# First attention stage: the next head's transposes moved to mid-head and to other PSUM banks, weightings placed between root tiles, three root tiles ahead of the log tiles

## The reference

```python
q, k = _l2norm(to_heads(q)), _l2norm(to_heads(k))
cos = jnp.einsum('bhsd,bhtd->bhst', q, k)
g_dist = jnp.arccos(jnp.clip(cos, -1.0 + EPS, 1.0 - EPS))
attn_score = (1.0 + g_dist) ** (-3.2)
n_r, n_c = jnp.sum(attn_score, axis=-1), jnp.sum(attn_score, axis=-2)
k_tilde = (n_r ** -1.0)[..., :, None] * attn_score * (n_c ** -1.0)[..., None, :]
probs = k_tilde / jnp.maximum(jnp.sum(k_tilde, axis=-1, keepdims=True), 1e-12)
out = jnp.einsum('bhst,bhtd->bhsd', probs, v)
```

## Time and profile before

| | |
|---|---|
| runs, us | 3973.3, 3965.14, 3962.1 (median 3965.14) |
| profiled execution, us | 3964.4 |
| its span, us | 3962.6 |
| mean granted TensorE clock | 0.802 |
| busy over the span | PE 80%, DVE 75%, ACT 80%, POOL 30% |

### The profile page before, as it was taken

One profiled execution on the slowest core, in us unless ns is written; L12 is line 12 of the kernel. 1 busy time (PEld: TensorE's weight loads), 2 busy tenths in 40 slices (PEclk: granted clock), 3 DMA queues, 4 the chain that ended last, 5 costly groups with the idle time before them and its releaser, 6 DMA issues. The chain is left out here.

```text
span 3962.6 us, 59670 instructions
## 1 busy us (share of the span) xinstructions
PE 3159.4 (80%) x18880; PEld 1315.8 (33%) x18880; DVE 2984.2 (75%) x4684; ACT 3180.3 (80%) x2658; POOL 1175.7 (30%) x746
## 2 busy tenths in 40 slices
PE   4777787778777877787777575888888888888899
PEld 2221122112211221122111232355555555555547
DVE  6777977797779777977797798878787787788411
ACT  2699999999999999999998564488788787888822
POOL 2111011101110111011100043477677676777700
PEclk8776677667766776677667698799999999999999
DMA  1000000000000000000000135011001000110000
GB/s 38 32 7 7 0 6 6 6 0 6 6 6 2 5 6 6 4 3 6 6 5 5 35 124 154 22 39 28 23 23 44 23 23 23 39 28 23 18 19 11
DMA packets 59591, 86.13 MB, mean 22 GB/s; under 512 B 9808, under 2 KB 45904, under 8 KB 58960
## 3 DMA queue, kind: packets, MB, share of 16 engines
q1 hardware_dynamic: 59344, 83.06, 7.4%
HBM read 52.44 MB, written 30.54 MB: 21 GB/s over the span
## 5 line engine op out<-in xcount | busy, mean ns | idle before, releaser
L1089 POOL TENSOR_TENSOR lo<-pr,hi 128x1024 f16<-128x1024 f32 x384 | 916.7, 2412 | 396.9 <-ACT hi L1215 394.8
L1138 DVE TENSOR_REDUCE mx<-mx_ps 128x1 f32<-128x512 f32 x1024 | 660.1, 684 | 175.1 <-PE mx_ps L1253 171.8
L660 PE MATMUL r_ps<-qst,kst 72*128 72x512 bf16 x1024 | 575.6, 565 | 252.2 <-DVE wt L470 188.9
L1230 ACT ACTIVATE pr<-s_ps 128x1024 f32<-128x1024 f32 x512 | 531.6, 1038 | 275.4 <-PE s_ps L1274 243.8
L664 PE MATMUL r_ps<-mst 110*128 110x512 f16 (+1 forms) x1024 | 512.7, 507 | 81.5 <-DVE wt L451 35.4
L1215 ACT ACTIVATE hi<-pr 128x1024 f16<-128x1024 f32 x512 | 547.3, 1070 | 0.0
L287 POOL COPY mono_x<-two 128x256 f32 (+1 forms) x16 | 8.5, 530 | 1781.4 <-PE t_ps L633 1727.9
L1253 PE MATMUL mx_ps<-ka,qa 128*128 128x512 f16 x1024 | 385.3, 397 | 139.3 <-DVE mx L1138 116.4
L589 ACT ACTIVATE wt<-wt 128x2048 f32<-128x2048 f32 x256 | 484.6, 1895 | 0.0
L580 ACT ACTIVATE wt<-wt,theta_bias 128x8192 f32<-128x8192 f32 x64 | 453.6, 7111 | 0.2
L1293 PE MATMUL pv_ps<-vh,hi 128*128 128x129 f16 x4096 | 434.2, 223 | 11.3 <-ACT sums L1221 5.8
(11 more groups left out here) (179 smaller groups left out, 4302.6 us busy)
## 6 DMA issues: line engine op xcount, KB each, us to landing
qk<-stg SPq DMA_DIRECT2D x6, 2048.0 KB, 13.6
vh<-v SPq DMA_DIRECT2D x16, 520.0 KB, 3.6
qa<-qk SPq DMA_DIRECT2D x16, 512.0 KB, 3.7
ka<-qk SPq DMA_DIRECT2D x32, 256.0 KB, 4.8
v<-v_st SPq DMA_DIRECT2D x3, 2080.0 KB, 7.9
qst<-parts_dram SPq DMA_DIRECT2D x144, 32.0 KB
kst<-parts_dram SPq DMA_DIRECT2D x144, 32.0 KB
qk<-stg SPq DMA_DIRECT2D x4, 1024.0 KB, 8.3
```

Of the source, the lines that this page charges most:

```text
L660: mm = eng.matmul(r_ps[:, r % 2, :], kst[:, cols(k)], qst[:, cols(n_, BANK)], start=True, stop=True)
L1089: eng.tensor_tensor(lo[:, i % NHL, :, :], pr_slot(i), hi[:, i % NHL, :, :], ALU.subtract).then_inc(lo_done, 1)
L1138: eng.tensor_reduce(mx4[:, q // NCH, q % NCH:q % NCH + 1], mx_ps[:, q % 2, :], AX.X, ALU.max)\
L1230: eng.activation(pr_slot(i), s_ps[:, i % 2, :, :], ACT.Exp, scale=SM).then_inc(exp_done, 1)
```

## The change

It moves work between places of each engine's order, in the first attention stage alone; no instruction is taken out, and ScalarE gets two more `theta` calls a head (six groups where there were four, over the same tiles).
- **Order of tiles.** The ring and VectorE take three root tiles, then the eight log tiles, then five root tiles (before: four, eight, four).
- **Factors.** `turn_factors` writes into `m_ps`, whose two halves are free between a head's last square and the next head's first; so its 32 transposes no longer wait for VectorE's copies one by one. They stand behind the tenth ring chunk of the fourth root tile. `turn` stands behind the tenth chunk of the third root tile of the next head.
- **Weightings.** Places 0, 1 and 2 stand behind the tenth ring chunk of root tiles 5, 6 and 7 (the last three, counted from 0); places 3 to 8 between the ring's end and `start`; places 9 to 13 behind `start`; 14 and 15 open the next head, as before.
- **VectorE.** `values` of places 0 to 3 stands behind root tile 4, that of places 4 to 7 behind root tile 6. The four `stack` copies follow root tile 7. `finish` and `finish_rows` of the head before move to the third root tile.
- **Theta groups** are of 4, 4, 5, 1, 1 and 1 tiles.
- **`ring_to`** is worked out from other constants.

```diff
+    RA = 3
+    GROUPS = (0, 4, NL, NL + 5, NT - 2, NT - 1, NT)
+    PAIRS = tuple(range(0, NL, 2)) + (NL,)
...
-    ROOT_US, CHUNK_US, HALF_US = 1.035, 0.69, 1.24
+    ROOT_US, CHUNK_US, CUBE_US, LOAD_US, LAG_US = 0.954, 0.625, 2.35, 1.3, 1.2
...
-        st_ps = t_ps[:, :, :].rearrange("p a b -> p (a b)").bitcast(F16)
+        st_ps = m_ps[:, :, :].rearrange("p a b -> p (a b)").bitcast(F16)
...
                     if not first:
-                        values(h - 1, NT - 2, 2)
-                    for j in range(QH):
+                        values(h - 1, NT - 2, 1)
+                        values(h - 1, NT - 1, 1)
+                    for j in range(RA):
+                        if j == RA - 1 and not first:
+                            finish(h - 1)
                         root_tile(h, j)
+                    if not first:
+                        finish_rows(h - 1)
                     for j in range(NL):
                         log_tile(h, j)
-                    for j in range(QH, NQ):
+                    for j in range(RA, NQ):
                         root_tile(h, j)
-                    if not first:
-                        finish(h - 1)
-                    values(h, 0, GROUPS[1])
-                    values(h, GROUPS[1], NL - GROUPS[1])
-                    if not first:
-                        finish_rows(h - 1)
+                        if j == NQ - 4:
+                            values(h, 0, GROUPS[1])
+                        if j == NQ - 2:
+                            values(h, GROUPS[1], NL - GROUPS[1])
                     if not last:
                         for j in range(4):
                             stack(h + 1, j)
-                    values(h, NL, QH)
-                    values(h, NL + QH, QH - 2)
+                    values(h, NL, GROUPS[3] - NL)
+                    values(h, GROUPS[3], NT - 2 - GROUPS[3])
...
                     for r in range(done, NRING):
                         ring(h, r)
-                    if not first:
-                        turn(h - 1)
-                    for p in range(NL):
-                        weigh(h, p)
-                    if not last:
-                        for j in range(4):
-                            turn_factors(h + 1, j)
-                    for p in range(NL, NL + QH):
+                        if r == q_at(RA - 1) + 9 and not first:
+                            turn(h - 1)
+                        if r == q_at(RA) + 9 and not last:
+                            for j in range(4):
+                                turn_factors(h + 1, j)
+                        for p in range(3):
+                            if r == q_at(NQ - 3 + p) + 9:
+                                weigh(h, p)
+                    for p in range(3, NL + 1):
                         weigh(h, p)
                     if not last:
                         start(h + 1)
-                    for p in range(NL + QH, NT - 2):
+                    for p in range(NL + 1, NT - 2):
                         weigh(h, p)
```

More of the change, by code:

```diff
@@ L324, in stage_attention0 @@
     NCU = 2 * NQ
[L325 removed]
+    NSG = len(PAIRS) - 1
     def q_at(j):
[L328 removed]
+        return 12 * j if j < RA else 12 * j + 4 * NL
     def s_at(j):
[L331 removed]
+        return 12 * RA + 4 * j
     def place(tile):
@@ L337, in tile_of @@
         return NQ + p if p < NL else p - NL
-    ROOT_US, CHUNK_US, HALF_US = 1.035, 0.69, 1.24
-    LOAD_US = 1.3
-    TILE_US = 12 * CHUNK_US + 2 * HALF_US
+    ROOT_US, CHUNK_US, CUBE_US, LOAD_US, LAG_US = 0.954, 0.625, 2.35, 1.3, 1.2
     def ring_time(r):
[L345 to L352, removed]
+        q, z = (r, 0) if r < s_at(0) else (s_at(0), r - s_at(0)) if r < s_at(NL) else (r - 4 * NL, 4 * NL)
+        return (q + z) * CHUNK_US + (q // 12 + (q % 12 >= 8)) * CUBE_US
     def root_time(g):
         return ROOT_US * g + (LOAD_US if g >= 2 * NQ else 0.0)
-    ring_to = [sum(1 for r in range(2, NRING) if ring_time(r - 1) <= root_time(g)) + 2 for g in range(NM0)]
+    ring_to = [2 + sum(1 for r in range(2, NRING) if ring_time(r - 1) + LAG_US <= root_time(g)) for g in range(NM0)]
     with ExitStack() as ctx:
@@ L550, in _ @@
                 head(H - 1, last=True)
-                values(H - 1, NT - 2, 2)
+                values(H - 1, NT - 2, 1)
+                values(H - 1, NT - 1, 1)
                 finish(H - 1)
@@ L601, in _ @@
                     for g in range(NSG):
-                        pair = wt[:, NQ + 2 * g:NQ + 2 * g + 2, :]
+                        pair = wt[:, NQ + PAIRS[g]:NQ + PAIRS[g + 1], :]
                         if g == 0:
@@ L606, in _ @@
                     for g in range(NSG):
-                        pair = wt[:, NQ + 2 * g:NQ + 2 * g + 2, :]
-                        eng.wait_ge(ring_read, NRING * h + s_at(2 * g + 2))
+                        pair = wt[:, NQ + PAIRS[g]:NQ + PAIRS[g + 1], :]
+                        eng.wait_ge(ring_read, NRING * h + s_at(PAIRS[g + 1]))
                         eng.activation(pair, pair, ACT.Arctan, scale=1.0 / (GQK * GQK)).then_inc(atan_done, 1)
                     eng.preload_act_table_set("natural_log_exp_and_others")
[L611 to L620, removed]
+                    for p in range(-1, NT):
+                        if p == -1:
+                            theta(h, 0)
+                            theta(h, 1)
+                        elif p in (GROUPS[1], GROUPS[3] - 1, GROUPS[4] - 1):
+                            theta(h, 2 + (GROUPS[1], GROUPS[3] - 1, GROUPS[4] - 1).index(p))
+                        elif p == NT - 1:
+                            theta(h, 5)
+                        if p >= 0:
+                            score(h, p)
             @block.tensor
@@ L681, in turn @@
                     eng.wait_ge(o_copied, h + 1)
-                    if not (isinstance(h, int) and h == H - 1):
-                        eng.wait_ge(mst_ready, 4 * (h + 2))
                     for j in range(4):
```

25 lines of the change are left out of this document (11 added, 14 removed).

## The result

The changed kernel takes 3974.5 us (median of 10 runs, 3969.6 to 3979.9) against 3964.4 for the kernel before (10 runs, 3958.3 to 3973.3). The ratio is 1.0025, 95% interval 1.0014 to 1.0036: 10 us slower where 3965 and no change was forecast. That is inside the range, but the interval leaves out 1: the kernel did become slower.

The account below looks back on a forecast made before the run. ScalarE was taken as the bound, working 122.3 of 131.04 us a head; -45.6 + 7.5 + 37.5 + 4.5 - 5 - 4 + 5.7 = +0.6 us gave 3965 us, range 3941 to 3994.

Parts of the forecast that it names:

- the table `ring_to`: Ring chunks on PE one square later, so the Ln of the log tiles waits less on PE: -5 us.
- Arctan: ScalarE's wait ahead of the last two Arctans falls from 3.9 to about 1.0 a head: gain 45.6 us.
- ahead of the Sqrts, head 0, and small gaps: Head 0's transposes no longer wait for copies, so its squares start at 120.1 instead of 124.19: -4 us.
- PE behind the last Exp: After the last head's last Exp, PE has 13 places left, ending 8.2 after it instead of 2.5: +5.7 us.
- The end of the head: Later ring end and weightings on PE lengthen the waits ahead of first and third Sqrt: losses of 7.5 and 37.5 us.
- VectorE's wait: VectorE stands idle 4 to 6 us on the Exp of place 3, ahead of root tile 5.
- the margin: VectorE's last root tile is ready only 0.9 us before ScalarE wants it for the last `theta`; no wait there.
- Mid-tile work: PE's transposes and single weightings amid tiles mostly hidden; 0.1 charged per weighting, 4.5 us in all, bounds 0 and 0.5 each.
- six `theta` calls cost what four did: On ScalarE, two more `theta` calls a head cost next to nothing.
- The slower chain: Rival: time lost in last root tiles, ring, weightings or squares behind VectorE's wait returns each head: 3985 us, chance 0.37.
- the third rival: VectorE isn't ready for the log tiles by the first Sigmoid, giving back up to 46 us: 4010 us, chance 0.03.
- The earlier clock rise: Rival: PE's clock is up at the ring's end, six weightings take 5.5 us: 3938 to 3948 us, chance 0.2.

Follow-up runs that it names:

- the second experiment: Changed kernel with `values` of places 0 to 3 behind root tile 5 instead of 4, weightings 0 and 1 amid root tiles 6 and 7: 3906.1 us.
- The first experiment: Changed kernel with the `ring_to` table moved one square earlier, nothing else: 3952.6 us, ratio 0.997 to the kernel before.

## Where the forecast was wrong, and where it was right

The forecast was no change, with the remark that less than 12 us can't be told from none. The kernel became 10 us slower, and ten runs of each tell that from none. The main terms held. The step that failed stands among the small terms: the table `ring_to` was to shorten the Ln's waits by 5 us, and it lengthened them by 11.7.

| us over the stage | forecast | measured | from |
|---|---|---|---|
| ahead of Arctan | -45.6 | -43.5 | 63.6 to 20.1 |
| ahead of the Sqrts, heads 1 to 15 | +49.5 | +45.4 | 57.0 to 102.4 |
| ahead of the Sqrts, head 0, and small gaps | -4 | -9.4 | the rest of 70.6 to 106.6 |
| ahead of Ln | -5 | +11.7 | 17.0 to 28.7 |
| ScalarE's own work | 0 | +6.3 | busy 1959.1 to 1965.4 |
| PE behind the last Exp | +5.7 | +6.1 | 2.5 to 8.6 |
| sum | +0.6 | +16.6 | |

The 49.5 is 7.5 + 37.5 + 4.5. Read directly, the stage ends 17.2 us later (2234.7 to 2251.9). The rest of the program, which is not touched, took 5 us less in this one profile (1727.9 to 1722.9); among the kernels shown here it lies between 1714 and 1733. Over ten runs each the medians differ by 10. So the total came nearer than its terms, partly by luck: the Ln and ScalarE's work missed by 23.0 us one way, the Sqrts and head 0 by 9.5 the other, and the rest of the program took off some more.

- **Arctan: right.** VectorE starts the log tiles 3.73 after the first Sigmoid began (557.37 - 553.64), before 6.52: 2.79 earlier, against 2.85. The rest is 1.23, against 1.0.
- **The end of the head: right in the mechanism and in what stands there after.** Forecast were waits of 1.15 and about 5.75 a head; 1.22 and 5.61 came. The six weightings took 7.52 (7.25), the squares' start to the third Sqrt 8.20 (8.3). The 0.66 + 3.25 taken for the kernel before is 57.0 / 15 = 3.8 over all heads. Only the 4.5 us for work inside the tiles did not come.
- **VectorE's wait: right in place and size** (3.93 against 4 to 6), and so was the margin: no wait ahead of the last `theta`. The `values` behind root tile 6 took 0.87 (627.45 to 628.32) instead of 0.5. That the wait is the path, and not only a risk to it, is shown by the second experiment.
- **Mid-tile work: nearer its lower bound of nothing.** A weighting takes 1.94 and leaves PE idle for 0.40, and root tiles 5 and 6 keep 10.4 (606.79 to 617.21). The transposes cost VectorE 1.07, ahead of its wait.
- **The failed step: the small term of the table `ring_to`.** I wrote that each chunk one square later should let the Ln wait less on PE, -5 us. It waited more: +11.7, and the Ln's busy time rose too. I had looked at which instruction stands ahead of a square on PE, and not at the clock at which both run. The first experiment undoes this one line and takes back 21.9 us, twice the difference between the kernels: with the earlier spacing the changed kernel is 12 us faster than the kernel before. What sets the clock there stays open, and the second experiment's heads show that this table does not cost the same in each of them.
- **The second, smaller one: "six `theta` calls cost what four did".** From start to start a call takes 8.72 for 10240 columns (606.07 to 614.79) and 1.90 for 2048 (629.93 to 631.83), so nearly 0.2 of each is the start itself; the last one, whose own Exp waits for it, takes 2.01. The six take 28.56 a head, where four of 7.01 took 28.04: 0.5 a head, 8 us over 16 heads, of which the ledger keeps 6.3. In the kernel with the transposes alone the six groups cost some 22 us, waits included; their waits in the changed kernel were not taken apart. I had set the Arctans of the earlier trace rows beside them, 7.14 for two, and those carry no `theta_bias`. Their starts are 3.52 apart, and 4096 columns at the pace of `theta` are 3.41, so an Arctan's start costs about 0.1. The Trainium skill, ScalarE: Activation LUTs, section What ACT_TABLE_LOAD costs, states that each operand of one value per partition adds about 93 ns to an ACTIVATE; with nearly 0.2 for a `theta` and 0.1 for an Arctan the trace agrees.
- **The rivals.** The slower chain was named for tiles or weightings that lose time. They didn't; the 10 us came from elsewhere. (Its chance, 0.37, and the 0.03 of the third rival, counted within slower, make 0.40, where the numbers have 0.38.) The earlier clock rise did not come with single weightings: six places took 7.52, not 5.5. The log tiles were in time.

**What the change really is.** The transposes alone bring 3.5 us a head (131.5 to 128.0). All of the rest together costs 5.0 (128.0 to 133.0), although 2.6 of Arctan's wait are gone with it. My sum priced the end of the head as one chain, and so could not show that one part of the change earns 52 us (3965.4 to 3913.0) and the rest, on top of it, loses 62 (to 3974.5).

## What to carry to other kernels

When work is moved to an earlier place, look at what the engine in between then waits for: VectorE's 3.93 us for an Exp, three tiles ahead of the head's end, came out nearly in full as two waits of ScalarE. A table that spaces one engine's work over another's has to be judged by the clock that it leaves, not only by the order: here one square of spacing moved 22 us in the changed kernel and 6 in the one with the later `values`. And try each part of a large change alone, since two of its parts can hide what a third is worth.

## What the runs showed of the hardware

**VectorE and GpSimd hold each other up.** In the changed kernel, two VectorE passes with both inputs in SBUF (line 456), beside GpSimd's last factors:

```profile
596.75 1.90 POOL L305 TENSOR_TENSOR mono_p<-mono_p 128x448 f32<-128x448 f32 x1
598.73 2.12 POOL L307 TENSOR_TENSOR fac<-mono_p,fac 128x576 f16<-128x576 f32 x1
```

The VectorE row is the one of 596.35 above: 3.38 for two passes that take 2.35 elsewhere in the same head. GpSimd's two took 1.90 and 2.12, against 0.93 and 1.27 with no such pass beside them. The Trainium skill, SBUF — State Buffer, section Who interferes with whom, says that such a pair excludes each other, and the trace agrees. It cost ScalarE nothing here, since VectorE waits 3.93 behind it.

**The clock follows what is laid around the work.** The six weightings behind the ring took 1.25 us a place; four behind a pair took 0.91, and two behind an idle of 3.91 took 1.7 each, all with the same matmuls. The seven behind the ring in the second experiment took 7.45 in one head and 8.72 in another.

**A head has a period of its own.** The changed kernel's heads in the loop are 133.1 or 133.2 long; the kernel before alternates from its third head on between 131.06 and 131.75, and several experiments do so too. I did not test what a head takes over from the one before it.
